# Other places for the units, turns and products of an attention pair on TensorE

## The chip, the cores and the metric

The kernel runs on one core of a Trainium2 chip. The metric is the device time of one execution in microseconds, the median of several runs; less is better. Engines are named as in the profile: PE is TensorE (PEld its weight loads), DVE VectorE, ACT ScalarE, POOL GpSimd, SP the engine that only issues DMAs here.

## The reference

Two sequences of 2048 tokens with 256 features go through half a feed-forward block, causal attention with 16 heads, and the same half feed-forward block again. Cut to what matters:

```python
x = x + 0.5 * ffn(layernorm(x), k0, k1, k2, s0, s1, s2)   # three layers with weights +1 or -1, relu
x = x + attention(layernorm(x), w_q, w_k, w_v, w_o, b_o)
x = x + 0.5 * ffn(layernorm(x), k0, k1, k2, s0, s1, s2)

# attention: b=2, s=2048, 16 heads of 16
scores = einsum('bhqd,bhkd->bhqk', q, k) / sqrt(16)
scores = where(k later than q, -1e9, scores)
attn = softmax(scores, axis=-1)
ctx = einsum('bhqk,bhkd->bhqd', attn, v)
return ctx.reshape(b, s, 256) @ w_o.T + b_o
```

## The kernel before, in words

Three stages follow each other. The first does the first feed-forward block and the projections, chunk by chunk of 512 tokens, and writes q, k and v to DRAM (qk_scr, v_scr). The second is the attention, and the only one that the change touches. The third adds the attention and does the second feed-forward block.

The attention works on pairs of heads: 8 pairs for each of the 2 sequences, 16 in all, numbered 0 to 15. The queries of a pair are four chunks of 512, numbered 0 to 3. Chunk i needs the keys up to its own end, and is worked in 2i + 2 steps of two key blocks of 128 and two heads. That makes STEPS = 20 steps a pair (s0, s1 for chunk 0; s2 to s5 for chunk 1; s6 to s11 for chunk 2; s12 to s19 for chunk 3) and four scores blocks a step (j = 0 to 3).

TensorE gets its whole order written out (L1337 to L1346). For each step g and each j it does:

- `scores(g, j)` (L1291): four matmuls of 32 columns each (tiles 128x32) fill one of three PSUM banks; it waits until ScalarE has done the exp of the block three before (L1298). ScalarE then writes probs (L1277).
- `max_pass` (L1326): work for the maximum over the keys, which the softmax needs before the scores of a chunk can be made. A *unit* (t, r) is the scores of 128 queries against up to 512 keys for both heads (L659, tiles 64x128), with four small matmuls for the mask on the diagonal (L665). VectorE reduces it (L680). Two PSUM places are used in turn, so that unit or turn number n waits for VectorE's work on number n - 2 (L652). When the last unit of a chunk is reduced, VectorE forms the negative maximum (L684), GpSimd splits it into two float16 parts (L694 to L698), and the *turn* of that chunk (L669) transposes them; VectorE copies the result to m_row (L688), and SP writes it as two more rows of q (`sp_rows`, L700, two DMAs).
- `products(g - PV_LAG)` (L1306): eight matmul records of 32 columns, the products of the step three before with v (L1321). After the last step of a chunk ScalarE copies the sum to ctx_out (L1263, L1267), and SP stores it (L1188). ctx_out has two halves, used in turn; the copy waits until the store of two copies before has landed (L1266).

The units and turns of a pair are not done inside that pair alone. They form a list of 44 (PERIOD, L578 to L583) that starts in the pair before: the entries with d = 0 belong to the pair that runs, those with d = 1 to the next one. Three tables set the places:

- PV_POINTS[s]: after which scores block of step s the products stand. The same table sets the place of ScalarE's copy (L1279) and of SP's store (L1213) in those engines' queues.
- ITEM_POINTS[n]: the place of list entry n, as 8 s + 2 j, plus 1 if it stands behind the products of that j. It orders TensorE, VectorE, GpSimd and SP alike.
- TURN_DELAY[i]: how many units after the last one of chunk i its turn stands in the list.

A place is written s8.2 for s = 8, j = 2.

SP's queue is one sequence too (L1195 to L1215). At a turn it issues the two rows; at turn 2 it goes on with the loads of the next pair, after a wait for all products of the pair before, and in four pairs with two reads of the context:

```python
if x == ("turn", 2):
    wait(sp, se.pv_done, pair * STEPS)
    if last:
        load_ctx(sp, 0, 1)
    else:
        load_pair(sp, 1 - pair % 2, pair + 1)
    if pair in FIRST_LOAD_PAIRS:
        for sem in ctx_st:
            sp.wait_ge(sem, 8 * PAIRS * QCH)
        load_ctx(sp, 0, 0, (ctx_first, wgt_first), sc.first_in, [FIRST_LOAD_PAIRS.index(pair)])
```

`load_pair` (L307) is 16 DMAs of q and k (L313, L314) and one of v (L315); FIRST_LOAD_PAIRS are pairs 9 to 12 (L610), and their reads are L545. The store of a finished chunk stands at steps 2, 4, 8 and 14: at s2 that of the last chunk of the pair before, then those of chunks 0, 1 and 2. The first unit of the next pair (entry 17 of the list) waits for the loads (L1334). In the last pair the entries with d = 1 are left out, and the output projection of the third stage's first chunk stands at s13 to s15 (L1345).

Of the kernel before, what the change touches and what calls it, by code (L numbers as in the profile page):

```python
# [57 lines left out]
ST_BANKS, P_SLOTS = 3, 4  # L58
PV_LAG = 3

PV_POINTS = (2, 2, 2, 3, 0, 0, 1, 3, 3, 3, 3, 1, 2, 0, 1, 0, 2, 2, 2, 0)

TURN_DELAY = (2, 7, 4, 3)


ITEM_POINTS = (8, 8, 18, 21, 24, 27, 27, 32, 36, 38, 46, 47, 52, 56, 60, 63, 66, 70, 77, 77, 79, 81, 81, 90,
               91, 97, 97, 102, 103, 107, 111, 118, 119, 125, 128, 128, 138, 138, 142, 146, 147, 151, 159, 159)


class LayerNormSems:  # L70
# [186 lines left out]
def build(nc, x, w_q, w_k, w_v, w_o, b_o, k0, k1, k2, s0, s1, s2, out):  # L257
# [8 lines left out]
    with ExitStack() as top:  # L266
# [269 lines left out]
        def load_ctx(sp, b, i, to=(ctx_in, wgt_in), done=sc.ctx_in, parts=range(2 * DT)):  # L536

            for a in range(2):
                for hf in range(DT):
                    if a * DT + hf not in parts:  # L540
                        continue
                    src = ctx_scr.rearrange("(b q) (h a e) n -> b a (q h) e n", b=BATCH, h=2, a=2)[
                        bass.ds(b, 1), a, hf * 8:(hf + 1) * 8, :, bass.ds(i * CH, CH)].rearrange("o g e n -> (o g) e n")
                    for dst, e in zip(to, (0, DK)):
                        sp.dma_start(dst[:, a, hf, :], src[:, e:e + DK, :]).then_inc(done, 16)  # L545
# [33 lines left out]
        for n in range(2 * UNITS):  # L579
            PERIOD.append((n // UNITS, units[n % UNITS]))  # L580
            due += [(n + TURN_DELAY[i], n // UNITS, i) for i in range(QCH) if last_unit[i] == n % UNITS]
            PERIOD += [(d, ("turn", i)) for at, d, i in due if at == n]
        PERIOD = PERIOD[PERIOD.index((0, units[LEAD])):PERIOD.index((1, units[LEAD]))]  # L583
        AHEAD = [x for d, x in PERIOD if d == 1]
        assert len(PERIOD) == S_USES and len(ITEM_POINTS) == S_USES and S_USES % 2 == 0

# [27 lines left out]
        def items(pair, s, j):  # L614

            found, use = [], len(AHEAD) + pair * S_USES
            for (d, x), point in zip(PERIOD, ITEM_POINTS):
                if pair + d == ALL_PAIRS:
# [559 lines left out]
        with ExitStack() as st:  # L1178
# [8 lines left out]
            def _(sp):  # L1187
# [7 lines left out]
                for pair in range(ALL_PAIRS):  # L1195
                    last = pair == ALL_PAIRS - 1
                    for s in range(STEPS + (PV_LAG if last else 0)):
                        g = pair * STEPS + s
                        for j in range(4):
                            for _, owner, x, use in items(pair, s, j) if s < STEPS else ():  # L1200
                                if x[0] == "turn":
                                    sp_rows(sp, owner % 2, x[1], use)
                                if x == ("turn", 2):
# [5 lines left out]
# [4 lines that stand above are left out]
                            if j == PV_POINTS[s % STEPS] and g in ends:  # L1213
                                n = ends.index(g)
# [44 lines left out]
            def _(act):  # L1259
# [3 lines left out]
                def evacuate(n):  # L1263

                    wait(act, se.pv_done, ends[n] - PV_LAG + 1)
                    wait(act, ctx_st[n % 2], n // 2 * 16)  # L1266
                    nc.scalar.activation(ctx_out[:, n % 2, :], ctx_ps[:, :], ACT.Copy).then_inc(se.ctx_done, 1)  # L1267

                for g in range(ALL_STEPS):
                    s = g % STEPS  # L1270
                    for j, (kb, h, c0) in enumerate(step_slots(s)):
                        k = 4 * g + j
                        if k == 4 * (P_SLOTS - 1):
# [4 lines left out]
                                             scale=scale_now).then_inc(se.exp_done, 1)  # L1278
                        if j == PV_POINTS[s] and g in ends:  # L1279
                            evacuate(ends.index(g))  # L1280
# [3 lines left out]
            def _(pe):  # L1284
# [21 lines left out]
                def products(g):  # L1306

                    pair, s = divmod(g, STEPS)
                    i = chunk_of[s]
                    start = s == first_step[i]  # L1310
                    final = s + 1 == STEPS or chunk_of[s + 1] != i
                    if s == 0:
                        wait(pe, v_in[pair % 2], (pair // 2 + 1) * 16)
                    if start:
                        wait(pe, se.ctx_done, pair * QCH + i)
                    if diagonal(s):
                        wait(pe, se.mask_done, pair * (QCH * TPC) + i * TPC + 2 * (s - first_step[i] - 2 * i) + 2)
                    wait(pe, se.exp_done, 4 * g + 4)
                    for j, (kb, h, c0) in enumerate(step_slots(s)):
                        row = 32 * (2 * h + kb % 2)  # L1320
                        ins = nc.tensor.matmul(ctx_ps[row:row + 32, c0:CH], v_buf[pair % 2][:, kb, h * 32:(h + 1) * 32],  # L1321
                                               probs[:, g % P_SLOTS, j, c0:CH], start=start, stop=final,
                                               tile_position=(0, row))
                    ins.then_inc(se.pv_done, 1)

                def max_pass(pair, s, j, after):  # L1326
                    for late, owner, x, use in items(pair, s, j):
                        if late != after:
                            continue
                        if use == len(AHEAD):  # L1330
                            pe.wait_ge(sb.s_done, len(AHEAD))
                            pe.wait_ge(sa.v_ev, NCH * 2)
                        if owner != pair and x == units[0]:
                            load_wait(owner % 2, owner // 2)  # L1334
                        pe_item(owner % 2, x, use % 2, use - 1, owner * QCH + x[1] + 1 if x[0] == "turn" else None)

                for g in range(ALL_STEPS):  # L1337
                    pair, s = divmod(g, STEPS)
                    for j in range(4):
                        scores(g, j)  # L1340
                        max_pass(pair, s, j, 0)
                        if j == PV_POINTS[s] and g >= PV_LAG:
                            products(g - PV_LAG)
# [173 lines left out]
```

## Time and profile before

| | us |
|---|---|
| median of 3 runs | 1563.32 (1562.93 to 1565.04) |
| profiled execution, own time | 1563.57 |
| its span | 1561.8 |
| PE busy | 1537.2 (98%) |
| DVE busy | 1122.0 (72%) |
| ACT busy | 840.8 (54%) |
| share of PE in the chain that ended last | 96% |
| attention stage | about 452 to 1201 |

The profile is one execution. Times in rows are in microseconds from the start of the span. In a timeline consecutive instructions of a line are merged into one row: start, length, engine, line, operation, output<-input, shapes, count, and in brackets the engine's idle time before it with what ended it. The length of a matmul row holds the time in the pipeline, so that rows of PE overlap; the distance from one start to the next tells what the engine really needs.

### The profile page before, as it was taken

What the parts mean: (1) busy time and instruction counts of PE and PEld (TensorE: products, weight loads), DVE (VectorE), ACT (ScalarE), POOL (GpSimd) and SP (SyncE); (2) the same over time, 40 slices, a digit from 0 to 9 for tenths busy, and PEclk for the clock granted to TensorE, in tenths of its full rate; (3) what the DMA queues carried; (4) which work ended last, traced back from release to release, by engine and by line L of the source; (5) the groups of instructions that cost most, each with busy time, mean ns of one, the idle gap of its engine ahead of it and who ended that gap; (6) DMA issues with size and microseconds to landing.
All of it is one profiled execution on the core that took longest, in us unless ns stands there. A gap on an engine that the chain in (4) does not pass through costs nothing.

```text
span 1561.8 us, 35447 instructions
## 1 busy us (share of the span) xinstructions
PE 1537.2 (98%) x14112; PEld 724.3 (46%) x14112; DVE 1122.0 (72%) x1616; ACT 840.8 (54%) x1703; POOL 194.5 (12%) x516
## 2 busy tenths in 40 slices
PE   6999999999989999999999999999999999999998
PEld 3555555555443343343333333334333555555554
DVE  6535543554658999989989999999996667666552
ACT  3223322322158888888888888888886222222221
POOL 4300000000011122121122121112220000000000
PEclk9999999999999999999999999999999999999999
DMA  5121023202041222211222212222210222211210
GB/s 172 28 68 54 13 67 91 71 13 67 2 125 46 70 63 69 63 36 49 70 70 63 81 44 62 73 83 63 70 71 27 81 68 71 76 49 59 81 27 14
DMA packets 146227, 96.39 MB, mean 62 GB/s; under 512 B 106544, under 2 KB 125616, under 8 KB 146096
## 3 DMA queue, kind: packets, MB, share of 16 engines
q1 hardware_dynamic: 146096, 94.54, 21.3%
q8 instruction: 94, 1.54, 0.4%
q14 instruction: 37, 0.30, 0.1%
HBM read 49.15 MB, written 37.75 MB: 56 GB/s over the span
## 4 chain that ended last, share of the span: by engine, by line
PE 96%; ACT 1%; SPq 1%; DVE 1%; DMA 1%; issue 0%; ACTq 0%; DVEq 0%
PE ffn_mm L437 28%; PE ffn_mm L1301 18%; PE ffn_mm L1321 16%; PE ffn_acc L453 7%; PE ffn_mm L423 7%; PE ffn_acc L659 6%; PE ffn_tr L659 5%; PE ffn_mm L754 4%; PE ffn_acc L568 2%; PE ffn_acc L766 2%; ACT probs L1277 1%; PE ffn_tr L407 1%; PE ffn_tr L665 1%; PE ffn_acc L665 0%; DMA v_scr<-v_pad 0%
## 5 line engine op out<-in xcount | busy, mean ns | idle before, releaser
L1277 ACT ACTIVATE probs<-ffn_mm 128x512 f32<-128x512 f32 (+3 forms) x1280 | 597.6, 544 | 117.3 <-PE ffn_mm L1301 108.2
L680 DVE TENSOR_REDUCE m_part<-ffn_acc 128x2 f32<-128x1024 f32 (+1 forms) x348 | 370.0, 1063 | 37.2 <-PE ffn_acc L659 31.9
L1301 PE MATMUL ffn_mm<-qk 128*32 128x512 f16 (+7 forms) x5120 | 386.9, 354 | 6.3 <-ACT probs L1277 5.3
L437 PE MATMUL ffn_mm<-ffn_h1h,w 128*128 128x512 f16 x1024 | 388.3, 379 | 0.0
L437 PE MATMUL ffn_mm<-ffn_h1l,w 128*128 128x512 f16 x1024 | 388.1, 379 | 0.0
L680 DVE TENSOR_REDUCE m_part<-ffn_tr 128x2 f32<-128x1024 f32 (+2 forms) x292 | 308.6, 1057 | 37.9 <-PE ffn_tr L659 25.7
L1321 PE MATMUL ffn_mm<-probs,v 128*32 128x512 f32 (+3 forms) x2560 | 306.1, 536 | 0.0
L503 ACT ACTIVATE ffn_h2h<-ffn_mm 128x512 f16<-128x512 f32 x128 | 76.4, 597 | 296.2 <-PE ffn_mm L437 294.7
L1301 PEld LDWEIGHTS ffn_mm<-qk 66*32 66x32 f16 (+1 forms) x5120 | 135.1, 94 | 212.1 <-ACT probs L1277 116.0
L514 DVE SCALAR_TENSOR_TENSOR ffn_h2l<-ffn_mm,ffn_h2h 128x512 f16<-128x512 f32 x128 | 85.7, 687 | 166.7 <-ACT ffn_h2h L503 166.7
L437 PEld LDWEIGHTS ffn_mm<-ffn_h1h,w 128*128 128x128 f16 x1024 | 100.2, 98 | 118.8 <-issue 1.8
L437 PEld LDWEIGHTS ffn_mm<-ffn_h1l,w 128*128 128x128 f16 x1024 | 100.3, 98 | 117.8
L503 ACT ACTIVATE ffn_h1h<-ffn_mm 128x512 f16<-128x512 f32 x128 | 76.0, 597 | 131.3 <-PE ffn_mm L423 131.3
L1229 POOL TENSOR_SCALAR_AFFINE_SELECT probs<-probs 128x256 f32<-128x256 f32 (+1 forms) x256 | 102.8, 422 | 301.9 <-ACT probs L1277 301.7
L659 PE MATMUL ffn_acc<-qk 64*128 64x512 f16 (+1 forms) x696 | 125.1, 354 | 0.7 <-DMA qk<-qk_scr 0.5
L423 PE MATMUL ffn_mm<-ffn_x,w 128*128 128x512 f16 x512 | 115.4, 384 | 3.1 <-DVE ffn_x L469 2.4
L453 PE MATMUL ffn_acc<-w,ffn_h2h 128*128 128x256 f16 x512 | 113.8, 273 | 0.3 <-DVE ffn_h2l L514 0.3
L453 PE MATMUL ffn_acc<-w,ffn_h2l 128*128 128x256 f16 x512 | 113.7, 273 | 0.0
L514 DVE SCALAR_TENSOR_TENSOR ffn_h1l<-ffn_mm,ffn_h1h 128x512 f16<-128x512 f32 x128 | 88.2, 692 | 32.0 <-ACT ffn_h1h L503 31.5
L659 PE MATMUL ffn_tr<-qk 64*128 64x512 f16 (+2 forms) x584 | 104.2, 352 | 0.0
L659 PEld LDWEIGHTS ffn_acc<-qk 64*128 64x128 f16 x696 | 36.8, 93 | 116.8 <-issue 112.1
L1321 PEld LDWEIGHTS ffn_mm<-probs,v 128*32 128x32 f32 x2560 | 72.0, 109 | 28.0 <-issue 5.1
(119 smaller groups left out, 1033.4 us busy)
## 6 DMA issues: line engine op xcount, KB each, us to landing
qk<-qk_scr SPq DMA_DIRECT2D x256, 64.0 KB, 2.6
ctx_scr<-ctx_out SPq DMA_DIRECT2D x64, 256.0 KB, 2.7
qk<-ctx_scr SPq DMA_DIRECT2D x56, 256.0 KB
v_scr<-v_pad SPq DMA_DIRECT2D x32, 256.0 KB, 3.7
v<-v_scr SPq DMA_DIRECT2D x16, 512.0 KB, 4.0
x_res<-L_attn_x SPq DMA_DIRECT2D x8, 512.0 KB, 3.9
qk_scr<-qk_hi SPq DMA_DIRECT2D x32, 128.0 KB, 1.9
qk_scr<-qk_lo SPq DMA_DIRECT2D x32, 128.0 KB, 1.9
```

The source lines that it names most:

```text
L423: ins = nc.tensor.matmul(f.mm[:, m % 4, :], w0[:, kt, m * P:(m + 1) * P], part[:, kt, :], start=(kt == 0 and part is f.xh), stop=(kt == DT ...
L437: ins = nc.tensor.matmul(f.mm[:, m % 4, :], w1[:, kt, m * P:(m + 1) * P], part[:, kt, :], start=(kt == 0 and part is f.h1h), stop=(kt == H ...
L453: ins = nc.tensor.matmul(f.acc[:, t // 2, t % 2 * D:(t % 2 + 1) * D], part[:, kt, t * P:(t + 1) * P], w2[:, kt, :], start=(kt == 0 and par ...
L503: nc.scalar.activation(dst[:, m, :], f.mm[:, m % 4, :], ACT.Relu).then_inc(hi, 1)
L514: nc.vector.scalar_tensor_tensor(out=dst[:, m, :], in0=f.mm[:, m % 4, :], scalar=0.0, in1=src[:, m, :], op0=ALU.max, op1=ALU.subtract).the ...
L659: ins = nc.tensor.matmul(s_ps[slot][:, h, 0:w], q_part(u, h, HEAD_ROWS[h], slice(t * P, (t + 1) * P)), k_part(u, h, HEAD_ROWS[h], slice(r ...
L680: nc.vector.tensor_reduce(m_part[u][:, t, :, r], s_ps[slot][:, :, 0:w], AX.X, ALU.max).then_inc(sb.s_done, 1)
L754: ins = nc.tensor.matmul(f.mm[:, j, :], w_t[:, j // DT, kt, j % DT * P:(j % DT + 1) * P], src[:, kt, :], start=(kt == 0), stop=(kt == DT - 1))
L1229: nc.gpsimd.affine_select(out=view, in_=view, compare_op=ALU.is_ge, fill=0.0, base=c0 - (kb - TPC * i) * P, pattern=[[0, 2], [1, w]], chan ...
L1277: nc.scalar.activation(probs[:, g % P_SLOTS, j, c0:CH], st_ps[bank(k)][:, c0:CH], ACT.Exp, scale=scale_now).then_inc(se.exp_done, 1)
L1301: ins = nc.tensor.matmul(st_ps[bank(k)][c:c + 32, c0:CH], k_part(pair % 2, h, rows, slice(kb * P + c, kb * P + c + 32)), q_part(pair % 2, ...
L1321: ins = nc.tensor.matmul(ctx_ps[row:row + 32, c0:CH], v_buf[pair % 2][:, kb, h * 32:(h + 1) * 32], probs[:, g % P_SLOTS, j, c0:CH], start= ...
```

## The change

The three tables get other values. The list keeps its 44 entries; the only ones that change their order are turn 3 and unit (2, 0) of the next pair, since TURN_DELAY[3] is 2 instead of 3. Each unit, turn, product, copy, store, mask and row write is still done once, at another place of its queue. Turn 2 moves from s3.0 to s1.3, turn 3 from s9.3 to s8.2, turn 0 from s11.1 to s10.2, turn 1 from s17.3 to s16.3. The products at s2 stay behind j = 2.

```diff
-PV_POINTS = (2, 2, 2, 3, 0, 0, 1, 3, 3, 3, 3, 1, 2, 0, 1, 0, 2, 2, 2, 0)
-
-TURN_DELAY = (2, 7, 4, 3)
-
-
-ITEM_POINTS = (8, 8, 18, 21, 24, 27, 27, 32, 36, 38, 46, 47, 52, 56, 60, 63, 66, 70, 77, 77, 79, 81, 81, 90,
-               91, 97, 97, 102, 103, 107, 111, 118, 119, 125, 128, 128, 138, 138, 142, 146, 147, 151, 159, 159)
+PV_POINTS = (3, 1, 2, 1, 1, 0, 3, 3, 2, 2, 2, 2, 3, 2, 2, 3, 3, 3, 3, 1)
+
+TURN_DELAY = (2, 7, 4, 2)
+
+
+ITEM_POINTS = (0, 0, 7, 12, 15, 19, 19, 26, 29, 31, 34, 39, 43, 47, 52, 55, 60, 67, 67, 69, 73, 73, 80, 81,
+               85, 88, 88, 98, 99, 103, 107, 111, 116, 119, 122, 123, 132, 133, 135, 140, 141, 145, 149, 151)
```

## Rows read from the trace of the kernel before

**Rows 1.** The page, busy time, share of the span and instructions

```profile
PE 1537.2 (98%) x14112; PEld 724.3 (46%) x14112; DVE 1122.0 (72%) x1616; ACT 840.8 (54%) x1703; POOL 194.5 (12%) x516
```

**Rows 2.** Windows: stretch, length, busy PE, PEld, DVE, ACT, POOL; clock, DMA, GB/s

```profile
689.17:735.28 46.11, 46.11 (x633) 18.33 (x629) 41.97 (x49) 38.92 (x85) 8.74 (x29) 1.00 0.21 60
```

**Rows 3.** Timeline of PE in pair 5: start, length, and what

```profile
696.59 1.06 PE L1321 MATMUL ffn_mm<-probs,v 128*32 128x512 f32 x8
...
701.30 0.39 PE L659 MATMUL ffn_tr<-qk 64*128 64x512 f16 x2
701.53 0.38 PE L659 MATMUL ffn_acc<-qk 64*128 64x512 f16 x2
701.84 0.62 PE L1301 MATMUL ffn_mm<-qk 66*32 66x512 f16 x8
702.28 1.03 PE L1321 MATMUL ffn_mm<-probs,v 128*32 128x512 f32 x8
703.14 0.39 PE L1301 MATMUL ffn_mm<-qk 66*32 66x512 f16 x4
703.47 0.34 PE L659 MATMUL ffn_tr<-qk 64*128 64x384 f16 x2
...
703.79 0.62 PE L1301 MATMUL ffn_mm<-qk 128*32 128x512 f16 x8
704.34 0.39 PE L659 MATMUL ffn_acc<-qk 64*128 64x512 f16 x2
...
708.76 0.62 PE L1321 MATMUL ffn_mm<-probs,v 128*32 128x256 f32 x8
...
734.57 0.39 PE L659 MATMUL ffn_tr<-qk 64*128 64x512 f16 x2
734.90 0.39 PE L659 MATMUL ffn_acc<-qk 64*128 64x512 f16 x2
```

**Rows 4.** Timeline of DVE in pair 5, one reduction of a full unit

```profile
702.88 1.21 DVE L680 TENSOR_REDUCE m_part<-ffn_acc 128x2 f32<-128x1024 f32 x1
```

**Rows 5.** Timeline of ACT and PE in pair 0

```profile
461.85 2.06 ACT L1277 ACTIVATE probs<-ffn_mm 128x512 f32<-128x512 f32 x4 [3.36 <-DMA v_scr<-v_pad]
...
462.50 0.62 PE L1301 MATMUL ffn_mm<-qk 128*32 128x512 f16 x4 [2.84 <-ACT probs L1277]
462.90 1.93 PE L1321 MATMUL ffn_mm<-probs,v 128*32 128x512 f32 x8
...
471.12 0.60 PE L1321 MATMUL ffn_mm<-probs,v 128*32 128x512 f32 x4
```

**Rows 6.** Windows in pair 0, columns as in rows 2

```profile
458.00:461.00 3.00, 1.47 (x17) 0.46 (x13) 2.69 (x5) 0.49 (x1) 0.00 (x0) 1.00 0.68 171
...
464.00:467.00 3.00, 3.00 (x24) 0.79 (x18) 1.16 (x1) 0.73 (x2) 0.00 (x0) 0.50 0.56 139
```

**Rows 7.** Timeline of ACT (a copy) and of SP's queue in pair 5

```profile
709.46 0.60 ACT L1267 ACTIVATE ctx_out<-ffn_mm 128x512 f32<-128x512 f32 x1
...
695.36 0.33 SPq L1190 DMA_DIRECT2D ctx_scr<-ctx_out  x1
...
697.04 0.39 SPq L313 DMA_DIRECT2D qk<-qk_scr  x1
...
706.36 4.05 SPq L1190 DMA_DIRECT2D ctx_scr<-ctx_out  x2
```

**Rows 8.** Stores behind loads: landing in pair 5; queue and landing in pair 10

```profile
DMA to landing us min/median/max: 4.3/4.3/4.3
...
928.31 0.39 SPq L313 DMA_DIRECT2D qk<-qk_scr  x1
...
939.19 2.50 SPq L1190 DMA_DIRECT2D ctx_scr<-ctx_out  x2
DMA to landing us min/median/max: 6.1/6.1/6.1
```

**Rows 9.** Waits in pair 7: waiter, line and releaser; total, times, longest

```profile
PE ffn_acc L659 <- DMA qk<-qk_scr: 0.5, 1, 0.5
```

## The prediction

> **What bounds the kernel now.** I read the page's busy times first [rows 1]: TensorE is busy 98% of the span. A busy TensorE here is a full queue, not a full array, so I went to the stretches. An attention pair (one of 16; numbered 0 to 15) takes 46.1 us: pair 5 runs from 689.17 to 735.28, with TensorE busy throughout, VectorE 42.0 and ScalarE 38.9 us [rows 2]. So TensorE's own order sets a pair, VectorE is close behind it, and ScalarE has some slack. Steps are written s0 to s19 and s8.2 is the place after the third scores block of s8. S is a scores block, U a unit of the maximum pass, T a turn, P the products of a step.
>
> The start-to-start distances on TensorE in pair 5 are so regular that they can be used as prices [rows 3]. S to S is 0.22 us (703.79 holds two, U follows at 704.34: 0.22 + 0.33). P to S is 0.86 (702.28 to 703.14). S to U is 0.33 (703.14 to 703.47), U to U 0.23 (701.30 to 701.53), U to S 0.31 (701.53 to 701.84). So each passage between the units' tiles (64x128) and those of scores and products (128x32) costs 0.10 us, going in or coming out.
>
> **The change, part by part.** Only three tables differ. No work is added or removed; units, turns and products move, and with them everything that other engines issue at those places.
>
> *Mode passages.* I wrote out the 144 operations of a pair in both orders. Before, 56 times a unit meets a score or a product; after, 60 times. That is +4 x 0.10 = +0.4 us a pair. By passages alone the kernel would be 16 x 0.4 = 6.6 us slower. The Trainium skill (TensorEngine Tiling (Array Packing), Key Properties) has it as a rule that changing the tiling mode drains TensorE, which speaks against the change; by that rule, the trace agrees, at 0.10 us a passage.
>
> *Waits for VectorE and ScalarE.* A unit must wait until the reduction two uses before it is done, and a reduction of 1024 takes 1.2 us [rows 4], four times the distance of two units. Where two units stand together the second is sometimes held: 0.33 us instead of 0.23 at 734.57 to 734.90 [rows 3]. Twelve such places in pair 5, a few of them for ScalarE's exps, exceed the undisturbed distances by 0.85 us in all. With reductions of that length laid end to end against the new places I find ten, 0.45 us in all (the largest at s15.1, 0.10). So -0.4 us. An ordinary pair thus stays within 0.05 us of 46.1; I take +0.03, for 14 pairs +0.5 us, bounds -1 and +2. The last pair has no units of a next one, waits for ScalarE in its second half, and gets two more passages (0.2) and 0.2 to 0.3 of waits: +0.5.
>
> *The first pair.* ScalarE waits there until 461.85 for the stores of v, and TensorE stands idle for 2.84 us, until s3.3 at 462.50 [rows 5]. The new order puts two more units (0.22 + 0.17, 8 instead of 6) and one P (0.86) ahead of s3.3, and its extra passages too; all of it disappears in that wait, as the first pair's later part gets shorter by it: -1.4 with the waits that fall away. After that idle time the granted clock falls from 1.00 to 0.50 for some 7 us [rows 6], its lower level of 1.2 GHz. From the P at 462.90 to the P at 471.12 pass 8.22 us, and the same stretch of pair 5, 696.59 to 702.28, takes 5.69 [rows 3, 5]; 0.18 of the P's own lateness included, the slow clock costs 2.7 us. With some 2 us less idle I expect it to stay up: -2.7, bounds -2.7 and 0.
>
> *Turn 2 and what hangs on it.* This is the part that decides. Turn 2 moves from s3.0 to s1.3. On SP's queue the next pair's 17 loads are issued right behind turn 2, and they wait for the last products of the pair before (P at s2.2). The store of the context that this P completes is issued at s2.2 too. Before, the store came first: the store at 695.36, then turn 2's rows, and loads from 697.04 [rows 7]. After, turn 2 is in s1, so the rows and all loads stand ahead of the store, and it is issued only behind them. Who waits: ScalarE's copy at s8 (ctx_out<-ffn_mm) writes the same half of ctx_out (every second store), so it must wait until that store has landed. Behind that copy in ScalarE's queue are the exps of s8.3 and later, and TensorE may run only three scores blocks ahead.
>
> When does it land? The loads can start once the P at s2.2 is seen to be done. Ahead of that P stand seven S of 512 columns (1.54 us), two of 256 and two of 128 (0.34, by their columns), five full units and a small one (1.2), two P (1.72), T (under 0.1), eight passages (0.8) and a held unit (0.1): it starts 5.75 us into the pair, and the engine that waits for such a P sees its end 0.70 after its start (708.76 to ScalarE's copy at 709.46 [rows 3, 7]): 6.45. Turn 2's rows are issued by then. Before, the loads began at 697.04 - 689.17 = 7.87 [rows 2, 7], so everything on SP comes 1.4 earlier. From the first load to the landing of a store issued just behind the loads pass 706.36 + 4.3 - 697.04 = 13.6 us in pair 5 [rows 7, 8], so it would land at 20.1. The copy at s8 is due 20.3 into the pair (709.46 - 689.17 before [rows 7]; after, the same addition up to s8.2 puts the P ahead of it at 19.60, and 0.70 more). So an ordinary pair just makes it, by 0.2. Pair 7, whose loads take 1.5 us longer than in pair 5, would be some 0.7 late, pair 14 some 0.2. But in pairs 9 to 12 two reads of the context for the last stage stand between loads and store, and the store lands 5.4 to 6.2 us after its issue. From first load to landing pass 939.2 + 6.1 - 928.3 = 17.0 in pair 10 [rows 8], and 16.7, 16.1 and 16.7 in pairs 9, 11 and 12, which repeat it. With 6.45 they land at 23.4, and 23.2, 22.6 and 23.2, late by 3.1, and 2.9, 2.3 and 2.9. Nothing covers this: after s9.1 TensorE's next block needs the exp of s8.3, which is queued behind the copy. Sum 11.2 + 0.9 = +12.1 us. Bounds: +4 (the stores land 2 us sooner since the store before the loads is gone) and +18 (ordinary pairs late by 0.4 each).
>
> *Loads of the next pair.* Their first use moves from 19.4 to 19.0 into the pair and they start 1.4 earlier; the one wait for them in pair 7 (0.5 [rows 9]) goes: -0.5.
>
> *The clock again.* Four new idle stretches of 2.3 to 3.1 us stand in pairs 9 to 12, as long as the 2.84 that preceded the fall in pair 0. Each may cost 2.7 more. I take two of four, +5.4, bounds 0 and +11. The rows of pair 0 do not say which idle stretch is enough. The Trainium skill (TensorE: Matmul & The Clock Gate, What's actually happening) says that the throttled state is the default and activity releases it; pair 0 agrees, and no row here shows the clock beside a gap amid dense work.
>
> Sum: 0.5 + 0.5 - 1.4 - 2.7 + 12.1 - 0.5 + 5.4 = +13.9. The profiled execution took 1563.57 (its span is 1561.8); that gives 1577.5 for it. The median of the runs, 1563.32, is 0.25 below it, so 1577.2.
>
> **The rivals.** *A: the stores are late, but the clock stays up in pairs 9 to 12*: 1577.2 - 5.4 = 1571.8. For it: TensorE is dense on both sides of each gap, where in pair 0 it was thin before it as well (busy 1.47 of 3 us in 458 to 461 [rows 6]). *B: it falls all four times*: 1582.6. *C, the other side: the stores land in time*, because the DMA engines are less loaded without a store shortly before the loads, or because the loads start sooner than 6.45. Then only the rest counts: 1563.3 + 0.5 + 0.5 - 1.4 - 2.7 - 0.5 = 1559.7, faster. It decides if a landing comes within 13.8 us of the first load in pairs 9 to 12, against 16.1 to 17.0 now; little speaks for it. *D: half late*, about 1.5 us in each of the four, no fall of the clock: 1559.7 + 6 = 1565.7 to 1568. *E: the passages are paid and nothing comes back*: the waits only move to other units, +0.4 x 14 = +5.4 on top, 1582.6 with the forecast's two falls; against it, each of the twelve held places ends with a reduction or an exp that the new places leave more room.
>
> **How the numbers follow.** Forecast (one to three falls of the clock, 1574.5 to 1579.9 and some spread): 0.50. A 0.17, B 0.13, C 0.07, D 0.08, E 0.05. The range 1567.5 to 1583.0 leaves out C, most of D and the upper ends of B and E. A measurement of this kernel can tell about 0.2% (3.1 us) from no change: slower 0.90, same 0.04 (C or D with the clock of pair 0 falling as before), faster 0.06 (C).
>
> **What would show it.** On SP the store of s2 behind the loads in every pair, and its copy's successor at s8 with idle time put down to that store, 2 to 3 us in pairs 9 to 12 only. Those four pairs 2 to 6 us longer than 46.1, the others within 0.1 of it. The granted clock at 1.00 in 461 to 467 and below 1.00 after about two of the gaps. Units held less often than before. If ordinary pairs differ from 46.1 by over 0.1, the prices are wrong; if pairs 9 to 12 do not, the landing is.

## The result, and the profile after

The changed kernel took 1578.2 us (median of 4 runs, 1576.26 to 1580.29), the kernel before 1563.1 us beside it (1561.98 to 1565.04): a ratio of 1.0098, 95% interval 1.0086 to 1.011. The profiled execution took 1576.26 us with a span of 1574.5 us, 12.7 us more than before's 1561.8.

First the page: the busy times and the chain that ended last.

```profile
PE 1539.9 (98%) x14112; PEld 710.0 (45%) x14112; DVE 1120.1 (71%) x1616; ACT 848.4 (54%) x1703; POOL 199.6 (13%) x516
...
PE 88%; SPq 5%; DMA 4%; ACT 1%; issue 1%; DVE 1%; ACTq 0%; DVEq 0%
```

TensorE is as busy as in [rows 1], but its share of the chain fell from 96% to 88%, and SP's queue and DMA, together 2% before, now hold 9%. The waits of ScalarE and TensorE over the whole span name the pair of them (line waited for, releaser, total us, times, longest):

```profile
ACT ctx_out L1267 <- DMA ctx_scr<-ctx_out: 14.4, 10, 3.1
...
PE ffn_mm L1301 <- ACT probs L1277: 15.5, 13, 3.1
```

Before, the copy of the context (ctx_out) never waited for a store, and TensorE waited 5.3 us in 8 places for exps. Now ten copies wait, 14.4 us in all, and TensorE's waits grow by 10 us. Next, busy times by stretch: pair 4 (an ordinary pair), pair 5, and pairs 9 to 12 (columns as in [rows 2]: us, then PE, PEld, DVE, ACT, POOL busy with counts, granted clock, DMA share, GB/s):

```profile
639.81:685.78 45.97, 45.97 (x644) 17.39 (x632) 41.87 (x49) 39.34 (x84) 8.97 (x28) 1.00 0.21 60
685.78:733.24 47.46, 46.08 (x644) 17.31 (x632) 41.86 (x49) 39.45 (x84) 8.97 (x28) 1.00 0.20 58
...
872.16:922.42 50.26, 47.63 (x640) 17.66 (x632) 41.88 (x49) 39.55 (x84) 8.97 (x28) 0.97 0.21 65
922.42:970.51 48.09, 46.24 (x640) 17.29 (x632) 41.88 (x49) 39.45 (x84) 8.97 (x28) 1.00 0.24 68
970.51:1020.98 50.47, 47.64 (x640) 17.66 (x632) 41.88 (x49) 39.55 (x84) 8.97 (x28) 0.97 0.22 64
1020.98:1070.13 49.15, 46.07 (x640) 17.31 (x632) 41.86 (x49) 39.44 (x84) 8.96 (x28) 1.00 0.23 66
```

The ordinary pair is 45.97 us, 0.14 less than in [rows 2]. Pairs 9 to 12 are 50.26, 48.09, 50.47 and 49.15 us long, and two of them ran part of their time at the lower clock (0.97 is a mean over 50 us). In pair 9 the timeline of SP's queue and of the two engines behind it shows the whole sequence. It answers to [rows 7, 8]:

```profile
878.56 0.32 SPq L313 DMA_DIRECT2D qk<-qk_scr  x1
...
886.81 0.42 SPq L315 DMA_DIRECT2D v<-v_scr  x1
887.35 1.15 SPq L545 DMA_DIRECT2D ffn_h1h<-ctx_scr  x1
888.55 0.86 SPq L545 DMA_DIRECT2D ffn_h1l<-ctx_scr  x1
889.46 0.92 SPq L1190 DMA_DIRECT2D ctx_scr<-ctx_out  x2
...
895.25 0.60 ACT L1267 ACTIVATE ctx_out<-ffn_mm 128x512 f32<-128x512 f32 x1 [2.64 <-DMA ctx_scr<-ctx_out]
895.75 2.06 ACT L1277 ACTIVATE probs<-ffn_mm 128x512 f32<-128x512 f32 x4
896.39 0.40 PE L1301 MATMUL ffn_mm<-qk 66*32 66x512 f16 x4 [2.63 <-ACT probs L1277]
```

The loads begin 6.40 into the pair (predicted 6.45), the store is issued 17.3 into it, the copy that needs it stands idle for 2.64 us, and TensorE gets its next block 2.63 us late. The granted clock around that gap, in stretches of 3 us:

```profile
892.00:895.00 3.00, 1.76 (x33) 0.68 (x25) 2.54 (x4) 0.61 (x2) 0.01 (x1) 1.00 0.46 167
895.00:898.00 3.00, 1.61 (x18) 0.63 (x20) 0.46 (x2) 2.56 (x5) 0.59 (x3) 0.90 0.25 94
898.00:901.00 3.00, 3.00 (x32) 1.01 (x28) 1.56 (x2) 2.06 (x4) 0.24 (x1) 0.53 0.02 5
901.00:904.00 3.00, 3.00 (x55) 1.16 (x43) 2.10 (x3) 1.70 (x6) 0.98 (x3) 1.00 0.01 1
```

The clock falls to its lower level (1.2 GHz) at 897.38, about 1 us after TensorE has begun to work again, and comes back 3.4 us later. This is the profiled execution; the mean granted clock of the four executions was 0.995, 0.995, 0.997 and 0.993 (1576.26, 1578.68, 1577.71 and 1580.29 us), so they did not all have the same low stretches.

### The profile page after: what moved, and what is told of

The parts are those of the page before. It is cut to its first block, busy times and chain, and to the rows that moved or that the text cites. A ratio compares the mean times of both kernels' runs of the same rounds, so it can differ in the third digit from the quotient of the medians.

```text
span 1574.5 us, 35447 instructions
## 1 busy us (share of the span) xinstructions
PE 1539.9 (98%) x14112; PEld 710.0 (45%) x14112; DVE 1120.1 (71%) x1616; ACT 848.4 (54%) x1703; POOL 199.6 (13%) x516
## 3 DMA queue, kind: packets, MB, share of 16 engines
HBM read 49.15 MB, written 37.75 MB: 55 GB/s over the span
## 4 chain that ended last, share of the span: by engine, by line
PE 88%; SPq 5%; DMA 4%; ACT 1%; issue 1%; DVE 1%; ACTq 0%; DVEq 0%
PE ffn_mm L437 28%; PE ffn_mm L1301 15%; PE ffn_mm L1321 13%; PE ffn_mm L423 7%; PE ffn_acc L453 7%; PE ffn_acc L659 5%; PE ffn_tr L659 4%; DMA ctx_scr<-ctx_out 4%; PE ffn_mm L754 4%; SPq L313 2%; SPq L314 2%; PE ffn_acc L568 2%; PE ffn_acc L766 2%; ACT probs L1277 1%; PE ffn_tr L407 1%
## 5 line engine op out<-in xcount | busy, mean ns | idle before, releaser
L1277 ACT ACTIVATE probs<-ffn_mm 128x512 f32<-128x512 f32 (+3 forms) x1280 | 603.8, 543 | 113.2 <-PE ffn_mm L1301 99.7
L1301 PE MATMUL ffn_mm<-qk 128*32 128x512 f16 (+7 forms) x5120 | 391.1, 356 | 16.0 <-ACT probs L1277 15.5
L680 DVE TENSOR_REDUCE m_part<-ffn_acc 128x2 f32<-128x1024 f32 (+1 forms) x333 | 355.8, 1069 | 36.1 <-PE ffn_acc L659 27.1
L680 DVE TENSOR_REDUCE m_part<-ffn_tr 128x2 f32<-128x1024 f32 (+2 forms) x307 | 322.8, 1051 | 55.1 <-PE ffn_tr L659 37.0
L1301 PEld LDWEIGHTS ffn_mm<-qk 66*32 66x32 f16 (+1 forms) x5120 | 127.3, 95 | 195.4 <-ACT probs L1277 126.3
L1229 POOL TENSOR_SCALAR_AFFINE_SELECT probs<-probs 128x256 f32<-128x256 f32 (+1 forms) x256 | 107.6, 424 | 378.0 <-ACT probs L1277 376.3
L659 PE MATMUL ffn_acc<-qk 64*128 64x512 f16 (+1 forms) x666 | 119.9, 356 | 0.1
L659 PE MATMUL ffn_tr<-qk 64*128 64x512 f16 (+2 forms) x614 | 109.7, 353 | 0.8 <-DVE m_part L680 0.4
L659 PEld LDWEIGHTS ffn_acc<-qk 64*128 64x128 f16 x666 | 33.2, 93 | 122.0 <-issue 120.1
```

The source lines that it names most:

```text
L659: ins = nc.tensor.matmul(s_ps[slot][:, h, 0:w], q_part(u, h, HEAD_ROWS[h], slice(t * P, (t + 1) * P)), k_part(u, h, HEAD_ROWS[h], slice(r ...
L680: nc.vector.tensor_reduce(m_part[u][:, t, :, r], s_ps[slot][:, :, 0:w], AX.X, ALU.max).then_inc(sb.s_done, 1)
L1229: nc.gpsimd.affine_select(out=view, in_=view, compare_op=ALU.is_ge, fill=0.0, base=c0 - (kb - TPC * i) * P, pattern=[[0, 2], [1, w]], chan ...
L1277: nc.scalar.activation(probs[:, g % P_SLOTS, j, c0:CH], st_ps[bank(k)][:, c0:CH], ACT.Exp, scale=scale_now).then_inc(se.exp_done, 1)
L1301: ins = nc.tensor.matmul(st_ps[bank(k)][c:c + 32, c0:CH], k_part(pair % 2, h, rows, slice(kb * P + c, kb * P + c + 32)), q_part(pair % 2, ...
```

## Experiments

The first three ask what the late stores cost and why, the fourth what a passage costs, the next two where the gain of the ordinary pair comes from, the last two what is left in the first pair. Pair lengths are the distances between the first scores blocks of consecutive pairs in each trace. The kernel before ran beside every group, with medians from 1562.2 to 1563.2 us.

### The new order, with SP's store ahead of the loads

```diff
-                                if x == ("turn", 2):
-                                    wait(sp, se.pv_done, pair * STEPS)
...
+                            if s == 2 and j == 3:
+                                wait(sp, se.pv_done, pair * STEPS)
```

TensorE, VectorE, ScalarE and GpSimd keep the changed kernel's order; on SP the loads and the context reads stand at s2.3, behind the store of s2.

> The new order on every engine, but on SP the loads that hang on turn 2, and the two context reads with them, are issued at s2.3, behind the store of s2. Nothing else differs from the changed kernel. If the late store is the cause, no copy at s8 waits for a store any more, pairs 9 to 12 fall from 48.1 to 50.5 us to about 46.0, the odd long pairs (5, 6, 14) as well, and the kernel takes 1578.2 - 15.9 (copies held) - 3.0 (two falls of the clock) = about 1559.5 us, below the kernel before. Rival, the new places themselves cost (four more passages a pair and worse waits): the time stays above 1570. Rival, the loads now come too late for the first unit of the next pair at s8.1: pairs get a wait for the load there of 0.5 us or more.

Measured: 1558.53 us (1557.37 to 1559.51), ratio to before 0.9976 (0.9966 to 0.9985). So one change of place in SP's queue turns 1% slower into 0.24% faster: 19.7 us, which is the late stores and what follows from them. Pairs 5 and 9 of this run, in the windows view, are now alike:

```profile
685.27:731.23 45.96, 45.96 (x644) 17.41 (x632) 41.86 (x49) 39.34 (x84) 8.97 (x28) 1.00 0.22 60
869.19:915.15 45.96, 45.96 (x642) 17.37 (x632) 41.87 (x49) 39.34 (x84) 8.97 (x28) 1.00 0.25 71
```

No copy waits for a store any more. Pairs 9 to 11 take 46.0 to 46.2 us; pair 12 still takes 47.04, by a stall that is described at the end. In pair 9 the store leaves 7.05 into the pair and the loads start 0.4 later:

```profile
876.24 0.33 SPq L1190 DMA_DIRECT2D ctx_scr<-ctx_out  x1
876.61 0.43 SPq L313 DMA_DIRECT2D qk<-qk_scr  x1
```

In pairs 1 to 14 the next pair's first unit still starts at 18.97 without a wait: there the earlier loads bought nothing. Only in pair 0 does it now wait, for 1.1 us.

### The old order, with the store behind the loads

```diff
-                            if j == PV_POINTS[s % STEPS] and g in ends:
+                                    if pair:
+                                        n = pair * QCH - 1
+                                        store(n // QCH, n, n % QCH)
+                            if j == PV_POINTS[s % STEPS] and g in ends and s % STEPS != 2:
...
```

The three tables of before; only the store of s2 goes behind the loads (and the context reads).

> The old order with one edit on SP's queue: the store of s2 is issued behind the loads of turn 2 (s3.0) instead of ahead of them. If the late store explains the loss, this shows it without any of the new places, and in a larger dose, since the loads start 1.5 us later here: the store lands some 21.5 to 23 us into a pair where the copy at s8 is due at 20.3, and 25 us in pairs 9 to 12. Per pair 1.2 to 2.7 us lost, in pairs 9 to 12 about 4.6 and a fall of the clock on top: 1563 + 10 x 1.8 + 4 x 5.5 = about 1603 us, between 1590 and 1615. If the loss came from the new places on TensorE, this kernel stays within 2 us of 1563.

Measured: 1603.64 us (1602.92 to 1604.36), ratio 1.0262 (1.0241 to 1.0282). The mechanism alone, with none of the change's order on TensorE, costs 41 us. The changed kernel's loads start 1.4 us earlier into the pair (6.40 against 7.82), which is why it pays less: added up over the pairs, its copies start 15.9 us late, those of this run 33.5. TensorE's waits and ScalarE's, of this run (L1273 and L1307 are before's L1267 and L1301):

```profile
PE ffn_mm L1307 <- ACT probs L1283: 37.5, 21, 4.5
...
ACT ctx_out L1273 <- DMA ctx_scr<-ctx_out: 31.8, 15, 4.4
```

Ordinary pairs took 47.1 to 47.6 us (pair 7 50.1 and pair 14 48.7, where the store was later), pairs 9 to 12 51.4 to 53.4. TensorE's gaps in these four were 3.8 to 4.5 us, and the clock fell at each: in pair 11 before the gap had ended, at 1012.89, in the others up to 0.8 us behind its end. It also fell behind the gap of pair 7, which was 2.0 us, and not behind those of pairs 14 and 15, 2.4 and 2.7 us.

### The changed kernel, with only the context reads moved behind the store

```diff
-                                    if pair in FIRST_LOAD_PAIRS:
-                                        for sem in ctx_st:
-                                            sp.wait_ge(sem, 8 * PAIRS * QCH)
-                                        load_ctx(sp, 0, 0, (ctx_first, wgt_first), sc.first_in, [FIRST_LOAD_PAIRS.index(pair)])
...
+                            if s == 2 and j == 3 and pair in FIRST_LOAD_PAIRS:
+                                for sem in ctx_st:
+                                    sp.wait_ge(sem, 8 * PAIRS * QCH)
+                                load_ctx(sp, 0, 0, (ctx_first, wgt_first), sc.first_in, [FIRST_LOAD_PAIRS.index(pair)])
```

> The changed kernel, but in pairs 9 to 12 the two context reads are issued behind the store of s2 instead of ahead of it; the loads stay ahead. By the theory the landing in these pairs comes 2 us sooner, as in any other pair: they take 46.0 to 47.5 us instead of 48.1 to 50.5, no fall of the clock in them, and the kernel about 1578.2 - 11.1 - 3.0 + 4 x 0.5 = 1566 us. If it is the loads alone that delay the store, nothing changes: 1578.

Measured: 1561.01 us (1558.65 to 1561.94), ratio 0.9989 (0.9979 to 0.9998). With the 17 loads still ahead of the store, the copies' waits shrink to a tenth:

```profile
ACT ctx_out L1267 <- DMA ctx_scr<-ctx_out: 1.4, 5, 0.4
```

Against the changed kernel that is 17.2 us less, of 19.7 in all (15.5 us between the two profiled executions). Most of it hangs on the reads: pairs 9 to 12 were 14.1 us over the ordinary length in the changed kernel's profile and are 1.3 over it here, 12.8 us less where 12.1 were expected. The run beat its expectation by 5 us all the same. 2.6 us of that lie in pairs whose order is the same in both kernels: outside pairs 9 to 12 late copies held pairs 1 to 14 for 3.9 us there and for 1.9 here, and the last pair is 0.6 us shorter. 1.7 more are the difference between the medians and the profiled executions. The store is issued 14.6 to 16.0 into such a pair in both; it lands within 4 to 6 us, and whether that is late is decided by tenths. In pair 5, from the first load to the landing, 15.4 us pass in the changed kernel and 13.2 here. What makes the landings of one execution slower than another's stays open.

### Six passages more

```diff
-ITEM_POINTS = (0, 0, 7, 12, 15, 19, 19, 26, 29, 31, 34, 39, 43, 47, 52, 55, 60, 67, 67, 69, 73, 73, 80, 81,
-               85, 88, 88, ...
+ITEM_POINTS = (0, 2, 7, 12, 15, 19, 19, 26, 29, 31, 34, 39, 43, 47, 52, 55, 60, 67, 68, 69, 73, 73, 80, 81,
+               85, 88, 90, ...
```

The first experiment's kernel, with three couples of adjacent units taken apart: 66 passages instead of 60.

> As the run with the store first, with three of the places where two units stand together split by one scores block (s0.0, s8.1, s11.0): six more passages between the tile shapes a pair, none removed. With 0.10 us a passage and nothing given back: +0.6 us a pair, 9.6 in all less what the second units waited before (0.1 a pair): +8 us against that run, about 1567. If a passage costs nothing when engines wait anyway, or the distances are hidden, the two are equal.

Measured: 1565.79 us (1564.43 to 1566.99), ratio 1.0021 (1.0011 to 1.0031), 7.3 us above the first experiment. The ordinary pair is 46.50 us, 0.53 more, or 0.09 us a passage. That is the price of [rows 3], by an edit made for it, and the alternative, that a passage costs nothing, is out. (TensorEngine Tiling (Array Packing), Key Properties, of the Trainium skill says that a change of tiling mode drains TensorE; these runs agree in that each change costs time, at that price.)

### New places for units and turns, old places for the products

```diff
-PV_POINTS = (3, 1, 2, 1, 1, 0, 3, 3, 2, 2, 2, 2, 3, 2, 2, 3, 3, 3, 3, 1)
+PV_POINTS = (2, 2, 2, 3, 0, 0, 1, 3, 3, 3, 3, 1, 2, 0, 1, 0, 2, 2, 2, 0)
```

On the first experiment's kernel. The question was which table brings the 0.14 us that the changed kernel gains in an ordinary pair.

> The new places of units and turns with the products at their old places, and SP's loads behind the store of s2 as in the run before this one of that kind (1558.5 us, ordinary pair 45.97 us). Written out, this order has 64 passages between the tile shapes (56 before, 60 in the changed kernel) and 8 places where two units stand together (12 and 10). The changed kernel's ordinary pair came out 0.14 us shorter than before, although its four passages more cost 0.4: some 0.5 us of waits fell away. Theory: they fell away because the units are spread more evenly for VectorE. Then the pair here is 46.11 + 8 x 0.09 - 0.45, about 46.4 us, and the time 1564.5 us (1562 to 1567). Rival: they fell away because of where the products stand (ScalarE's exps are read later). Then the pair is about 46.11 + 8 x 0.09 = 46.8 us and the time 1571 us.

Measured: 1630.44 us (1629.03 to 1631.08), ratio 1.0433 (1.0416 to 1.0451). Neither theory: the ordinary pair is 50.70 us. The window of pair 5 and what TensorE waited for over the whole run:

```profile
707.89:758.59 50.70, 48.01 (x628) 17.57 (x629) 42.24 (x48) 39.97 (x86) 8.96 (x28) 1.00 0.23 54
...
PE ffn_mm L1301 <- ACT probs L1277: 20.4, 66, 0.7
PE ffn_tr L669 <- DVE m_part L680: 11.2, 16, 0.7
...
PE ffn_acc L669 <- DVE m_part L680: 5.3, 11, 0.5
PE ffn_acc L669 <- POOL m_col L698: 3.2, 5, 1.1
```

VectorE and ScalarE work about as long as in [rows 2], within 1.1 us; TensorE waits for both. Turns (L669), which never waited for more than 0.6 us in the changed kernel, are now held in every pair, for example here:

```profile
732.85 0.56 PE L1301 MATMUL ffn_mm<-qk 128*32 128x512 f16 x8
734.13 0.22 PE L669 MATMUL ffn_tr<-ident_h,m_col 128*16 128x128 f16 x1 [0.71 <-DVE m_part L680]
```

### The opposite: old places for units and turns, new places for the products

The same PV_POINTS line in the kernel before, the other way round.

> The kernel before with the products alone at their new places; units, turns and SP's order as before. 58 passages (+2) and 11 pairs of adjacent units (-1). Theory (units' spacing gives the gain): pair 46.11 + 0.2 - 0.05, about 46.25 us, time 1565 us (1563 to 1567), and the first pair stays near 52 us because it is the units put ahead of s3.3 that shorten it. Rival (the products' places give it): pair about 46.11 + 0.2 - 0.5 = 45.8 us, time 1558 us.

Measured: 1633.83 us (1632.83 to 1635.35), ratio 1.0453 (1.0435 to 1.047); ordinary pair 51.07 us, pair 0 53.61. Again neither expectation, and here it is mostly units that wait for VectorE:

```profile
PE ffn_acc L659 <- DVE m_part L680: 27.7, 61, 0.5
PE ffn_mm L1301 <- ACT probs L1277: 20.3, 52, 2.3
PE ffn_tr L669 <- DVE m_part L680: 11.0, 31, 0.5
```

What the two have in common shows when each distance on TensorE in pair 5 is set against its undisturbed price. What goes beyond the prices is called held time here:

| | passages | held, us | pair from 46.11 by these, us | measured, us |
|---|---|---|---|---|
| before | 56 | 2.33 | | 46.11 |
| changed kernel's order | 60 | 1.78 | 46.11 + 0.40 - 0.55 = 45.96 | 45.97 |
| new units, old products | 64 | 6.11 | 46.11 + 0.80 + 3.78 = 50.69 | 50.70 |
| old units, new products | 58 | 7.19 | 46.11 + 0.20 + 4.86 = 51.17 | 51.07 |

(For the changed order the distances are those of the first experiment's pair 5.) The last two columns agree because held time is defined as what the prices leave over; what the table shows is how the loss divides: 0.1 us a passage explains 0.8 and 0.2 us of the two losses, and waiting the other 3.8 and 4.9. So the gain belongs to neither table. My explanation, which no run isolates: a products block takes 0.86 us, as long as four scores blocks; where it stands decides how far apart in time the units around it come, and a table of units that is even with one set of products is uneven with another. My expectations did not lay the reductions and exps out against the mixed orders; they counted passages alone, and so missed by over 4 us a pair.

### The first pair: loads before the wait for the stores of v

```diff
                 sp.wait_ge(sa.qk_st, NCH * 128)
+                load_pair(sp, 1, 1, v=False)
                 sp.wait_ge(sa.v_st, NCH * 64)
...
```

On the first experiment's kernel: its pair 0 took 48.90 us, with TensorE waiting 1.1 us at 473.1 for the q and k of pair 1. At s2.3 of pair 0 only the load of v is left.

> The run with the loads behind the store of s2 (1558.5 us), and in addition the 16 loads of q and k for pair 1 are issued before SP waits for the stores of v in pair 0, instead of behind that wait and the rows of turn 2. In that run pair 0 took 48.9 us although the granted clock stayed at 1.00, and TensorE waited 1.1 us for q and k of pair 1 at 473.1 to 474.2. Theory: that wait goes and nothing else changes: pair 0 47.8 us, time 1557.4 us (1556.5 to 1558). Rival: the loads share the DMA engines with the stores of v, ScalarE's wait for those ends some 1 us later, and pair 0 and the time stay as they were, 1558.5 us or up to 1 us more.

Measured: 1559.79 us (1558.63 to 1561.83), ratio 0.998 (0.997 to 0.9989); pair 0 took 49.22 us. Neither expectation's mechanism: the stores of v were not slowed (ScalarE's wait for them is 2.1 us, 2.3 before this edit), and the wait for the loads is gone, but the rows of turn 2 now stand behind 16 loads. TensorE's waits from 452 to 480, and SP's queue:

```profile
PE ffn_mm L1303 <- DMA qk<-m_row: 1.5, 1, 1.5
...
457.59 2.10 SPq L313 DMA_DIRECT2D qk<-qk_scr  x1
...
466.73 1.29 SPq L705 DMA_DIRECT2D qk<-m_row  x2
```

It is the case's own fault over again, made by me: an issue moved forward in a queue, and another pushed behind it.

### The first pair: rows, then loads, then the wait

```diff
+            if v_st is not None:
+                sp.wait_ge(v_st, NCH * 64)
             sp.dma_start(v_buf[u][:, :, :], v_scr[bass.ds(pair, 1)]...
...
                 sp.wait_ge(sa.qk_st, NCH * 128)
-                sp.wait_ge(sa.v_st, NCH * 64)
...
```

> As the run with the loads behind the store of s2 (1558.5 us), but SP's wait for the stores of v in pair 0 stands only ahead of the load of v for pair 1: the rows of turn 2 and the 16 loads of q and k are issued before it. In the run before this one the loads alone were pulled ahead of that wait; they started at 457.6 instead of 463.4 us, but the rows of turn 2 came behind them, at 466.7 instead of 462.0, and TensorE waited 1.5 us for those rows in place of 1.1 us for the loads (pair 0 49.2 us). Theory: with the rows ahead of the loads both waits go, pair 0 takes 47.8 us and the time is 1557.4 us. Rival: the loads slow the stores of v that they now run beside, ScalarE's wait for these (2.3 us) grows by about 1 us and pair 0 stays at 48.9 us, time 1558.5 us.

Measured: 1556.94 us (1556.32 to 1558.89), ratio 0.9962 (0.9948 to 0.9976). Pair 0 took 47.70 us, as the theory said, with rows at 457.8 and loads from 459.8:

```profile
457.84 1.96 SPq L706 DMA_DIRECT2D qk<-m_row  x2
459.85 0.39 SPq L313 DMA_DIRECT2D qk<-qk_scr  x1
```

The granted clock fell in this pair 0, at 457.40 for 3.4 us, and the pair is the shortest all the same: ScalarE still waited 1.2 us for the stores of v behind it, which covers the slow work. This version has the lowest median here, 1.6 us below the first experiment's; the runs of the two overlap. Its pair 12, at 48.13 us, took back 1.1 us in the profiled execution, by a stall that is described below.

## Why the prediction came out right, point by point

Forecast 1577.2 us, measured 1578.2. The profiled execution is the fairer check, since the sum was made for one: 1577.5 against 1576.26. By terms:

| term | predicted, us | measured, us |
|---|---|---|
| 14 ordinary pairs, order on TensorE | +0.5 | -2.0 |
| pair 0 | -1.4 - 2.7 | -3.3 |
| stores late in pairs 9 to 12 | +11.2 | +11.1 |
| stores late elsewhere, pairs 1 to 14 | +0.9 | +3.9 |
| clock falls after the gaps | +5.4 | +3.0 |
| last pair | +0.5 | +1.2 |
| waits of before that go | -0.5 | -1.4 |
| start of the stage | 0 | +0.1 |
| sum | +13.9 | +12.6 |

*The late stores are right.* By the copies' starts pairs 9 to 12 were held 2.8, 2.2, 3.0 and 3.2 us against 2.9, 3.1, 2.3 and 2.9 (single pairs are off by up to 0.9, the sum by 0.1). Every link is in the rows above, and the first and third experiments take the cost away by SP's queue alone, the second brings it back without the rest.

*Ordinary pairs' stores were under-priced.* I took the landing of pair 5 before, 4.3 us [rows 8], for the store's new place. Its issue came where it was reckoned or earlier (15.74 into pair 5, reckoned 15.8; mostly about 15.0; only pair 2 was later, 15.97), but it landed up to 6.0 us after that. ScalarE's copy in pair 5:

```profile
707.61 0.60 ACT L1267 ACTIVATE ctx_out<-ffn_mm 128x512 f32<-128x512 f32 x1 [1.39 <-DMA ctx_scr<-ctx_out]
```

A margin of 0.2 us was too thin to forecast pair by pair (pair 7, named as late, was in time; pairs 2, 5, 6, 8, 13 and 14 were not); the bound of 0.4 late in each ordinary pair holds the 3.9. The last pair's +1.2 is for 0.9 us one more such copy.

*The order on TensorE.* Passages +0.4 is right (0.09 us each in the split units' run; 16 x 0.4 is 6.4, not the 6.6 written). Held time fell by 0.55 and not 0.4 us, so that an ordinary pair became 0.14 us shorter where I had +0.03: the term is mis-sized by 2.5 us, outside its lower bound of -1. The level was misread as well: I counted twelve places and 0.85 us in pair 5 before, where every distance against its price gives 2.33. The other two orders show how much the held time can be, 6 to 7 us.

*The first pair.* The stretch ahead of the stores of v took in more work, but the clock did not stay up. Nor had it fallen after the idle time, as I wrote of the kernel before: there it fell at 461.89, 0.6 us ahead of the end of TensorE's gap. In the changed kernel it fell at 457.06, and stayed low for as long as before (6.8 us). In the windows view, after and then the first experiment, which has the same order there and kept its clock:

```profile
455.00:458.00 3.00, 2.25 (x33) 0.85 (x33) 2.72 (x4) 1.84 (x7) 1.75 (x4) 0.84 0.85 213
458.00:461.00 3.00, 3.00 (x24) 0.55 (x20) 2.11 (x2) 2.10 (x4) 0.00 (x0) 0.50 0.67 167
...
455.00:458.00 3.00, 2.26 (x37) 0.88 (x35) 2.61 (x4) 2.06 (x7) 1.66 (x4) 1.00 0.86 219
458.00:461.00 3.00, 2.80 (x34) 0.69 (x30) 2.84 (x3) 1.79 (x4) 0.00 (x0) 1.00 0.68 172
```

The products of step 3 start 1.3 us later with the low clock, not 2.7, because part of the slow work lies where TensorE would have waited anyway: the first experiment, at full clock, waited 1.1 us there, the changed kernel not at all (ScalarE's wait for the stores of v is 2.3 us in the one and 0.6 in the other, 3.36 in [rows 5]). So two errors, a fall that I had ruled out and a price taken from a place without cover, nearly met. Nor is that 1.3 all gained where the clock stays up: the first experiment's pair 0 is 48.90 against 49.03, since its loads for pair 1 were late by 1.1.

*The clock in the gaps.* In the profiled execution two of four fell, pairs 9 and 11, as taken (a guess, and the rows gave no better). Each cost 1.5 us (4.29 - 2.77 and 4.50 - 2.97, pair length over 45.97 less the time held), not 2.7: the clock stayed low for 3.4 us here and for 6.8 in pair 0 before. The gap of pair 12, the longest of the four (3.1 us), was not followed by a fall, and in the second experiment one of 2.0 us was. What decides it stays open. (TensorE: Matmul & The Clock Gate, What's actually happening, of the Trainium skill calls the throttled state the default, released by activity. The traces agree so far: every low stretch in the attention began during or within 1.5 us after time in which TensorE was partly idle. They also show that the length of one gap doesn't tell whether it comes.)

*The errors' signs.* The other stores, pair 0 and the last pair came out 3.0, 0.8 and 0.7 us above their terms, the ordinary pairs, the falls and the waits of before 2.5, 2.4 and 0.9 us below. The closeness of the total is in part luck; what was sound is that the largest term was worked out place by place, and that the range allowed for the rest.

## What to carry to other kernels

When work moves between places of a schedule that several engines share, write out every queue for the new places, and for each DMA that changes sides with another ask who waits for the one now behind: here 17 loads and two reads that nobody was waiting for went ahead of one store that decided, and putting the two reads alone back behind it already gave 17.2 of the 19.7 us. A load that nobody waits for belongs behind a store that somebody does. And where tables place units and products together, tune them together: each half of this change alone costs over 4%.

## What the runs showed of the hardware

- The granted clock can fall without a long gap. In pair 0 of the changed kernel it fell at 457.06 after two stretches of 3 us with TensorE busy for 2.2 us each and no wait above 0.6 us. With the same order on TensorE it fell again in the third and the last experiment (456.99 and 457.40), and not in the first and the last but one. Where it fell in the attention it stayed low for 3.4 or 6.8 us.
- A store of 256 KB that was issued ahead of the loads landed 2.4 to 2.9 us later (the store of s2 in the first experiment). Issued behind 17 loads and two reads it landed 5.6 to 6.2 us after its issue (pairs 9 to 12 of the changed kernel), and 4.8 to 5.3 with the reads behind it (third experiment).
- In pair 12 TensorE stops for nothing that the trace shows: near s10.3 in the first, the third and the last two experiments, with seven of the eight records of one products block done, and for 0.2 us near s11.1 in the kernel before. In the last experiment (lines shifted by one):

```profile
1030.26 1.03 PE L1322 MATMUL ffn_mm<-probs,v 128*32 128x512 f32 x7
1032.91 0.62 PE L1322 MATMUL ffn_mm<-probs,v 128*32 128x512 f32 x1 [1.62 <-issue]
```

Pair 12 is longer than its neighbours by 0.5 us before, 1.1 in the first and third experiments, 0.8 in the run before the last and 2.2 in this one; in the changed kernel, with the units split and with the mixed tables it is not. No run here tests what it is, and it stays open.
